# Late weight units on an even table in a mixture-of-experts kernel, and one weight copy issued half a slot earlier

## What is computed

```python
x = x + xattn(layernorm(x), ctx_1024, ...)     # 8 x 256 tokens of width 256, 16 heads, context of 77
h = layernorm(x)
probs = softmax(h @ gate_w.T)                  # 8 experts
w, idx = top_k(probs, 2); w = w / sum(w)
for gup, dn, ce in experts:                    # gup 2048 x 256, dn 256 x 1024, ce = the token's weight
    g, u = split(h @ gup.T, 2)
    acc = acc + ce[:, None] * (silu(g) * u @ dn.T)
x = x + acc
```

## Time and profile before

| | |
|---|---|
| median of 3 runs | 572.75 us (571.85 to 573.26) |
| the profiled execution | 573.26 us |
| its span in the profile | 571.5 us |
| PE busy | 507.7 us, 89% |
| DVE busy | 387.7 us, 68% |
| ACT busy | 346.8 us, 61% |
| POOL busy | 274.2 us, 48% |

### The profile page before, as it was taken

How to read it: one execution, slowest core, us unless ns; L and a number is a source line. 1 busy time by engine, 2 the same in 40 slices (tenths; PEclk the granted TensorE clock), 3 DMA queues, 4 the chain that set the end, 5 groups by cost and what they waited for, 6 DMA issues and landing times.

```text
span 571.5 us, 12061 instructions
## 1 busy us (share of the span) xinstructions
PE 507.7 (89%) x3715; PEld 368.9 (65%) x3730; DVE 387.7 (68%) x801; ACT 346.8 (61%) x643; POOL 274.2 (48%) x347
## 2 busy tenths in 40 slices
PE   4695889999898987899699999999999999999970
PEld 3462556667565655534367897888888888777640
DVE  5437458889788844688277888886767767666551
ACT  1220578889789885274666777766656556555530
POOL 5006464664555553101314666665667555563244
PEclk9976799999999987588999999999999999999995
DMA  7556657767767634263564688867555465664123
GB/s 209 187 163 175 232 152 220 215 198 225 210 186 209 197 98 130 97 193 105 148 139 85 117 182 202 166 108 162 96 104 81 79 97 90 107 66 66 20 29 45
DMA packets 88089, 79.87 MB, mean 140 GB/s; under 512 B 49176, under 2 KB 73368, under 8 KB 87896
## 3 DMA queue, kind: packets, MB, share of 16 engines
q1 hardware_dynamic: 76512, 63.38, 40.6%
q0 software_dynamic: 11520, 15.74, 17.2%
HBM read 49.08 MB, written 22.41 MB: 125 GB/s over the span
## 4 chain that ended last, share of the span: by engine, by line
PE 67%; DVE 10%; DMA 7%; ACT 6%; issue 4%; SPq 4%; POOL 1%; ACTq 0%; DVEq 0%; POOLq 0%
PE bank L1396 27%; PE bank L1413 13%; PE bank L1185 4%; PE bank L1231 4%; PE bank L1217 3%; DMA x_parts<-WE 2%; PE bank L1425 2%; PE bank L1199 2%; PE bank L1240 2%; PE bank L1266 2%; PE bank L1254 2%; DVE FB L1121 2%; DVE FB L1117 2%; PE bank L1278 2%; PE bank L1300 2%
## 5 line engine op out<-in xcount | busy, mean ns | idle before, releaser
L1396 PE MATMUL bank<-FB,WE 128*128 128x0 bf16 x1440 | 187.7, 280 | 4.5 <-issue 2.7
L1396 PEld LDWEIGHTS bank<-FB,WE 128*128 x1440 | 136.1, 98 | 35.4 <-issue 4.6
L671 POOL DMA_INDIRECT out<-FB,slot_tok x60 | 100.5, 1674 | 91.0 <-DVE FB L1133 88.0
L1121 DVE TENSOR_TENSOR FB<-FB 128x512 bf16<-128x512 f32 x120 | 83.4, 695 | 48.7 <-ACT FB L837 47.3
L837 ACT ACTIVATE FB<-FB 128x512 bf16<-128x512 f32 x120 | 75.5, 630 | 64.9 <-DVE FB L1117 64.1
L1413 PE MATMUL bank<-FB,WE 128*128 128x0 bf16 x720 | 103.5, 280 | 2.6 <-DVE FB L1121 2.0
L1117 DVE TENSOR_TENSOR FB<-FB,bank 128x512 f32<-128x512 f32 x120 | 82.1, 684 | 32.0 <-ACT FB L831 30.2
L662 POOL DMA_INDIRECT FB<-x_parts,slot_tok x60 | 62.2, 1037 | 75.4 <-DMA FB<-FB 31.5
L831 ACT ACTIVATE FB<-bank 128x512 f32<-128x512 f32 x120 | 71.2, 593 | 31.2 <-PE bank L1396 28.6
L1413 PEld LDWEIGHTS bank<-FB,WE 128*128 x720 | 68.0, 98 | 21.2 <-issue 5.6
L595 POOL TENSOR_TENSOR WE<-FB,WE 128x256 bf16<-128x256 f32 x104 | 67.8, 679 | 22.2 <-ACT WE L702 22.2
(11 more groups left out here) (176 smaller groups left out, 635.7 us busy)
## 6 DMA issues: line engine op xcount, KB each, us to landing
FB<-w SPq DMA_DIRECT2D x26, 512.0 KB, 5.5
WE<-w SPq DMA_DIRECT2D x44, 256.0 KB, 3.4
WE<-q_parts SPq DMA_DIRECT2D x32, 200.0 KB
WE<-x SPq DMA_DIRECT2D x16, 256.0 KB, 5.0
q_parts<-FB SPq DMA_DIRECT2D x32, 128.0 KB
x_parts<-WE SPq DMA_DIRECT2D x20, 128.0 KB, 3.7
out<-WE SPq DMA_DIRECT2D x20, 128.0 KB, 5.2
q_parts<-WE SPq DMA_DIRECT2D x16, 128.0 KB
```

What stands on the lines that cost most here:

```text
L671: pool.indirect_dma_start(out=out, out_offset=bass.IndirectOffsetOnAxis(ap=slot_tok[:, c:c + 1].bitcast(U32), axis=0), in_=y_sb[c % 2], in ...
L1121: nc.vector.tensor_tensor(hT[k % 3][:, 1, :], hid[k % 2], hT[k % 3][:, 0, :], ALU.subtract).then_inc(lo_ready, 1)
L1396: ins = nc.tensor.matmul(to, wf[:, bass.ds(at + o, P)], xgT[s % 2][:, 2 * part + kc, :].shape_from_register(long[s % 2]), start=(z == 0), ...
```

## The change

Three things are changed in the code, and nothing in what is computed.

1. The tables. Before, the 25 units stood after k = 1, 2, 5 (slot 0), 11 (slot 1), then five, five, six and five units in slots 2, 3, 4 and 5; the last after k = 47, the last chunk of slot 5. Now seven stand in slot 0 (after each of its chunks 1 to 7) and three in each of slots 1 to 6, after chunks 1, 3 and 6; the last after k = 54, chunk 6 of slot 6. The high parts on ACT stand after the same chunks in slot 0, and after chunks 0, 3 and 5 in the others.
2. The new tables have 28 entries. The tests in ACT's and DVE's loops read only the first 25, and so does `due`.
3. `park_in` stands on SP ahead of all four turns of slot 7's tiles, where it stood between the first two and the last two.

```diff
-FILL = [FC * s + c for s, chunks in enumerate(((1, 2, 5), (3,), (1, 3, 5, 6, 7), (1, 3, 5, 6, 7), (1, 2, 3, 5, 6, 7), (1, 3, 5, 6, 7))) for c in chunks]
-FILL_HI = [k - 1 if k >= 2 * FC and k % FC == 1 else k for k in FILL]
+FILL = [*range(1, FC), *(FC * s + c for s in range(1, E) for c in (1, 3, 6))]
+FILL_HI = [*range(1, FC), *(FC * s + c for s in range(1, E) for c in (0, 3, 5))]
...
             for s in range(NS - 1):
+                if s == E - 2:
+                    park_in()
                 for half in range(2):
-                    if s == E - 2 and half == 1:
-                        park_in()
...
-                    if k in FILL_HI:
+                    if k in FILL_HI[0:len(LATE) - NU]:
...
-                    if k in FILL:
+                    if k in FILL[0:len(LATE) - NU]:
```

## The result

The changed kernel takes 587.55 us (median of 4 runs, 584.62 to 589.33), the kernel before beside it 572.3 us (570.31 to 573.26): a ratio of 1.0266, 95% interval 1.0212 to 1.032. It is slower, and 588.0 us was predicted.

What follows compares the result with a forecast made beforehand. PE was taken to bound the expert part without slack; a 14.0 us stall ahead of slot 7, plus 2.5 us for the clock, less 1.2 us from the tables, gave 15.3 us over 572.75 us: 588.0 us, range 582.0 to 593.5 us.

Steps and rivals of the forecast that it cites:

- The tables cost nothing, and win some 1.2 us: Moved units covered by PE's work; slot 4's first wait and some slack of slot 3 go: -1.2 us, 0 to -1.8.
- The end of the last unit and the cover: Copy's wait on SP ends at 398.8 us; slot 7's first matmuls stood at 399.80 us, so 1.0 us of cover.
- The first link: From the parked copy's issue on SP until POOL can issue gather 30: 7.9 us, ends 3.2 and 8.5 us.
- The other links: After gather 30: gather 31 follows in 1.3 us, lands after 3.1 us, turn 31 is in place after 2.7 us.
- the last link: Turn 31 until it is in place for slot 7: 2.7 us, upper end 3.0 us.
- The stall: PE stands still ahead of slot 7: chain of 15.0 us less 1.0 us cover, 14.0 us; ends 9.3 and 17.1 us.
- The clock: After PE's idleness slot 7 starts at half speed for 5.0 us: +2.5 us, between 1.7 and 3.4 us.
- The sum: 14.0 + 2.5 - 1.2 = 15.3 us over the median of before, 572.75 us, giving 588.0 us.
- A short chain: Rival: turns pass the copy or lose little to it; stall 9.3 us instead of 14.0 us, 582.9 us; chance 0.16.
- The clock stays low: Rival: slot 7 runs at the lower clock throughout, losing 8.3 instead of 2.5 us, 593.8 us; chance 0.06.
- Not slower: Rival: units in slots 2 to 5 cost PE time there and none where they now stand; 569.3 us, chance 0.02.
- What I put at nothing: Scatters behind POOL's held gather, which DVE's result of tile 22 needs, end about when slot 7 can start: nothing added.

Runs made afterwards that it cites:

- tables_only: Against the changed kernel: new tables kept, parked copy back between the first two and last two turns of slot 7's tiles; 580.6 us, ratio 1.0117.
- even_early: Against the kernel with new tables and the copy in its old place: an even table ending with chunk 46 in slot 5; 570.23 us, ratio 0.9992.
- copy_last_down: Against the changed kernel: copy behind all four turns, PE's wait for it moved to slot 7's first down; 571.29 us, ratio 1.001.
- wait_only: Against the changed kernel: only the wait for the units ahead of the turns, copy behind them, PE needing it at slot 7's first down; 582.39 us, ratio 1.0149.
- place_only: Against the kernel before: old tables kept, parked copy moved ahead of all four turns of slot 7's tiles; 573.86 us, ratio 1.0007.
- last_at_50: Against the changed kernel: last three units after chunks 48, 49 and 50 instead of 49, 51 and 54; 579.24 us, ratio 1.0143.

## Why the prediction was right, point by point

- **The tables cost nothing, and win some 1.2 us.** The first is right; the gain is not shown. In the first profile slot 3 went from 17.60 us to 16.60 us, the first `up` of slot 4, which stood 0.97 us, no longer waits, and slots 0 to 5 together take 1.1 us less than before (101.5 for 102.6 us, from the first `hidden` of slot 0 to that of slot 6). But tables_only, with the same tables, shows such a wait again (1.76 us) and takes 103.7 us for these slots, and even_early and copy_last_down are not faster: the gain is within what one execution differs from the next. That the first profile meets the -1.2 us is luck.
- **The end of the last unit and the cover.** Predicted at 398.8 us with 1.0 us left. Measured 392.56 us and 1.2 us (PE's last matmul ended at about 393.7 us); the place in time is the 5.3 us by which the whole expert part came earlier, and the 1 us won.
- **The first link, copy to gather 30: 7.9 us predicted, 6.1 us measured** (392.63 to 398.75 us). This is the term that was mis-sized. The turns do queue behind the transfer, but the copy landed after 5.3 us and not 6.4 us, and gather 30 followed 0.8 us after that landing, where I had put 1.5 us. POOL, held itself, issued nothing while the copy ran; whether that is why it was faster is not shown, and in tables_only, where POOL also issued nothing meanwhile, it took 7.2 us.
- **The other links.** Gather 31 came 1.3 us after gather 30 as predicted. From there to slot 7 lie 6.05 us (400.07 to 406.12 us) against 5.8 us. (The upper end of the last link, 3.0 us, was too low for the rows it names, which allow 4 us; the measured sum did not need it.) The stall: 14.0 us predicted, 12.4 and 12.6 us measured, within 9.3 to 17.1 us.
- **The clock: 2.5 us predicted.** 1.4 us in the first profile (half of 2.90 us, most of it the 2.78 less 1.49 us of the first `up`), 2.7 us in the second (half of 5.40 us). The range of 1.7 to 3.4 us held in the second only.
- **The sum.** 15.3 us predicted. The expert part grew by 13.0 and 14.5 us, the medians by 15.3 and 13.7 us. That the first median's difference meets the prediction to 0.1 us is chance: the stall was over-estimated by some 1.5 us, in the first profile also the clock by 1.1 us, and executions differ by some us ahead of slot 0, where it starts at 276.7 to 282.4 us in these profiles.
- **The rivals.** *A short chain* has its measure in wait_only (8.84 us of gap): with only the wait ahead the gap is near the rival's 9.3 us, and the changed kernel's is not. *The clock stays low* did not occur. *Not slower* needed 0.52 us per unit; copy_last_down and even_early show none. I gave both parts of the change one price and did not say what either costs alone. Together they cost more than their sum by the gaps: 2.13 us for the place, 7.25 us for the table, 12.4 and 12.6 us for both. The ratios in the same set point the same way (1.0007, 1.0117 and 1.0237), but the intervals of the last two overlap. The expert parts don't settle it: over before they are 4.4, 10.9 and 13.0 to 14.5 us, with more in place_only's than its place.
- **What I put at nothing.** The scatters behind POOL's held gather: DVE's result waited 11.02 us and was free at 405.41 us, 0.7 us ahead of PE. Right: what PE next needs of DVE was done at 406.49 us and used at 410.84 us, so 4.3 us were to spare.

By the Trainium skill (DMA: Bandwidth & Descriptors, "Queues, rings and completion order") a ring's descriptors are consumed in order; the traces agree, with all but six of the copy's 128 packets started before the turns' first, and with 5.7 us from a turn's issue to its gather behind the copy and 2.7 us without it.

## What to carry to other kernels

A DMA that must wait belongs behind everything on its queue that could go now: ask of each transfer moved forward what its wait holds up, and follow that through the other engines to the next thing that the bound engine needs. Moving it behind is free only if its own landing is not needed before: here that took a wait on PE two chunks later. Two edits can cost more together than their sum, as the gaps here do, when one moves a condition later and the other moves its waiter earlier; price them together, from the moment when the condition is met to the moment when the work is due. Evening out work that is already covered wins nothing, but the last piece's due time can be on the path even if its duration is not.

## What the runs showed of the hardware that was not expected

- The same 1 MB copy from HBM took 5.3 and 5.5 us in the two profiles of the changed kernel and 5.5 us in last_at_50, 5.7 us in wait_only, 6.0 us in place_only, 6.4 us in before and in copy_last_down, and 7.2 us in tables_only. What makes it longer is open: POOL issued gathers or scatters while it ran in wait_only and in before, and none in tables_only. The same chain of copy, turns and gathers took 13.5 us in the changed kernel, 15.8 us in last_at_50 and 17.8 us in place_only.
- Two turns queued behind the copy moved together: in the changed kernel the last packet of both had ended at 398.47 us, before gather 30 was issued at 398.75 us, so gather 31 followed 1.3 us later with no wait of its own.
- After almost the same stall of 12.4 and 12.6 us, half clock lasted 2.9 us in one execution and 5.4 us in the other. After shorter stalls of 6.83 us (last_at_50), 7.25 us (tables_only) and 8.84 us (wait_only) it lasted 4.5, 4.8 and 4.3 us; after 2.13 us (place_only) the clock did not fall, and the first `up` took 1.51 us. Half of each is what it cost, 2.1 to 2.4 us in these three, where 1 to 1.3 us were expected: a longer stall did not cost more clock.
